# A Mamba scan kernel: the gates of the first two tiles share one table visit, and GpSimd's products use three places

## What is computed

```
xz = x @ win.T;  u, z = split(xz)                      # 1024 channels each
u = silu(conv4(u) + bconv);  dbc = u @ wx.T            # dt, B, C (16 states)
delta = softplus(dt @ wdt.T + bdt)
h = exp(delta * A) * h + (delta * u) * B_t             # a scan along the sequence, per channel and state
y = sum over the 16 states of h * C_t + u * Dp
y = (y * silu(z)) @ wout.T
```

## Time and profile before

| | |
|---|---|
| median of 3 runs | 7396.75 us (7392.23 to 7411.33) |
| the profiled execution, own time | 7406.93 us |
| its span, first to last instruction | 7405.0 us |
| busy share of the span | PE 91%, DVE 93%, ACT 83%, POOL 94% |
| granted TensorE clock, mean | 0.97 of full speed |
| share of the DMA engines | 46% |

### The profile page before, as it was taken

One profiled execution on the slowest core, in us unless ns is written; L12 is line 12 of the kernel. 1 busy time (PEld: TensorE's weight loads), 2 busy tenths in 40 slices (PEclk: granted clock), 3 DMA queues, 4 the chain that ended last, 5 costly groups with the idle time before them and its releaser, 6 DMA issues. The chain is left out here.

```text
span 7405.0 us, 108355 instructions
## 1 busy us (share of the span) xinstructions
PE 6731.3 (91%) x32416; PEld 4032.0 (54%) x32416; DVE 6877.8 (93%) x9234; ACT 6119.9 (83%) x13078; POOL 6953.7 (94%) x3764
## 2 busy tenths in 40 slices
PE   8999999999999999989999898999999999998799
PEld 5555555555555555555555555555555555555455
DVE  7999999999999999999999999999999999999766
ACT  6888888888888888888888888888888888888545
POOL 6999999999999999999999999999999999999678
PEclk9999999999999999999999999999999999999899
DMA  5455444445444444544444455344445544443155
GB/s 172 127 156 156 111 145 146 135 129 159 135 123 141 134 135 127 152 135 117 141 138 131 126 153 144 106 145 137 135 127 146 152 105 144 136 127 108 51 180 171
DMA packets 565933, 1006.64 MB, mean 136 GB/s; under 512 B 96624, under 2 KB 208368, under 8 KB 557552
## 3 DMA queue, kind: packets, MB, share of 16 engines
q1 hardware_dynamic: 559616, 993.54, 45.7%
q10 hardware_dynamic: 5744, 6.29, 0.3%
HBM read 875.49 MB, written 124.11 MB: 135 GB/s over the span
## 5 line engine op out<-in xcount | busy, mean ns | idle before, releaser
L517 POOL TENSOR_TENSOR dBu<-Bb,du 128x1024 f32<-128x1024 f32 x2048 | 4793.0, 2363 | 6.2 <-DMA Bb<-bc_scratch 4.7
L656 ACT ACTIVATE scans<-delta,A 128x512 f32<-128x512 f32 x4096 | 2745.0, 696 | 238.0 <-DVE hC L1160 216.6
L1144 DVE TENSOR_TENSOR_SCAN scans<-scans,state,dBu 128x512 f32<-128x512 f32 x2016 | 2533.4, 1277 | 228.5 <-ACT scans L656 224.0
L1144 DVE TENSOR_TENSOR_SCAN dBu<-scans,state,dBu 128x512 f32<-128x512 f32 x1568 | 1955.0, 1258 | 5.2 <-ACT scans L656 5.2
L892 PE MATMUL yT<-ident,hC 128*128 128x128 f32 x9216 | 1403.6, 283 | 289.0 <-DVE hC L1160 287.4
L1160 DVE TENSOR_TENSOR hC<-scans,Cb 128x512 f32<-128x512 f32 x2304 | 1551.0, 677 | 8.0 <-PE yT L892 7.8
L529 POOL TENSOR_TENSOR hR<-dBu,Cb 128x512 f32<-128x512 f32 x1024 | 1304.5, 1274 | 222.0 <-DVE dBu L1144 221.5
L892 PEld LDWEIGHTS yT<-ident,hC 128*128 128x128 f32 x9216 | 1087.2, 145 | 581.0 <-DVE hC L1160 364.6
L603 ACT ACTIVATE turned<-bg,CT 128x128 f32<-128x128 f32 x3072 | 875.0, 370 | 246.1 <-PE bg L869 245.7
L885 PE MATMUL bg<-u,comb 128*128 128x512 f32 x2048 | 963.6, 597 | 50.8 <-ACT pre L616 49.9
L843 PE MATMUL bg<-hT,win_z 128*128 128x512 f32 x2048 | 977.8, 600 | 0.0
(11 more groups left out here) (147 smaller groups left out, 7899.5 us busy)
## 6 DMA issues: line engine op xcount, KB each, us to landing
comb<-pre_scratch SPq DMA_DIRECT2D x992, 256.0 KB, 4.6
Bb<-bc_scratch SPq DMA_DIRECT2D x256, 512.0 KB, 6.9
Cb<-bc_scratch SPq DMA_DIRECT2D x256, 512.0 KB, 7.1
win_u<-in_win SPq DMA_DIRECT2D x256, 256.0 KB, 4.7
win_z<-in_win SPq DMA_DIRECT2D x256, 256.0 KB, 2.7
pre_scratch<-pre SPq DMA_DIRECT2D x248, 256.0 KB, 3.7
comb<-comb_scratch SPq DMA_DIRECT2D x61, 1024.0 KB, 7.2
part_scratch<-pre SPq DMA_DIRECT2D x128, 256.0 KB, 2.0
```

Source lines behind the costliest of these rows:

```text
L517: pool.tensor_tensor(dBu[:, ring(g, q)], Bb[:, 2 * q:2 * q + 2, :], du[:, j % 2, :].unsqueeze(1).broadcast_to([P, 2, T]), ALU.mult).then_i ...
L656: act.activation(place(n)[:], delta[:, j % 2, :], ACT.Exp, scale=A[:, i // CH_DIR, j * N + n:j * N + n + 1]).then_inc(dA_made, 1)
L1144: nc.vector.tensor_tensor_scan(to, place(n)[:], dBu[:, ring(g, q), k, :], state[:, c:c + 1] if i % CH_SEQ else 0.0, ALU.mult, ALU.add).the ...
```

## The change

z gets a second place. The z of tiles 0 and 1 go through silu together in the visit at position 7, and the visit at position 15 is gone. For that Z1 is done at positions 4 and 5, not 9 and 10, and the pieces of O0 to O3 are laid out anew. GpSimd's four products of a tile share three places in turn, not four of their own. The place in SBUF that the fourth one had served a load of wmod in the prologue too; this load now goes to Cb[8:12], so in the prologue the queue waits for the last prologue step before it loads the fifth pair of C. Nothing else in SyncE's order moves.

```diff
-HC, HR = 4, NA
+HC, HR = 4, 3
 GENERAL = [
-    ("D1", (0,), 0), ("Z0", (1, 2), 1), ("O0", (2, 2, 3, 3, 4, 4, 5, 5), 0), ("O1", (6, 6, 7, 7, 9, 9, 10, 10), 0),
-    ("D2", (7,), 1), ("Z1", (9, 10), 1), ("O2", (11, 11, 12, 12, 13, 13, 14, 14), 0), ("D3", (15,), 1),
-    ("O3", (15, 15, 17, 17, 18, 18, 19, 19), 0), ("Z2", (17, 18), 1), ("U0", (20, 20), 1), ("U1", (21, 21), 0),
+    ("D1", (0,), 0), ("Z0", (1, 2), 1), ("O0", (2, 3, 3, 4, 5, 6, 6, 7), 0), ("Z1", (4, 5), 1),
+    ("D2", (7,), 1), ("O1", (8, 8, 9, 9, 10, 10, 11, 11), 0), ("O2", (12, 12, 13, 13, 14, 14, 15, 15), 0), ("D3", (15,), 1),
+    ("O3", (16, 16, 17, 17, 18, 18, 19, 19), 0), ("Z2", (17, 18), 1), ("U0", (20, 20), 1), ("U1", (21, 21), 0),
-GATED = {7: (("Z", 0),), 15: (("Z", 1),), 23: (("Z", 2),), 31: (("C", 0), ("Z", 3)), 39: (("C", 2), ("Z", 4)),
+GATED = {7: (("Z", 0), ("Z", 1)), 23: (("Z", 2),), 31: (("C", 0), ("Z", 3)), 39: (("C", 2), ("Z", 4)),
-        z = sb("z", [P, T])
+        z = sb("z", [P, 2, T])
-        wgain = hR
+        wgain = Cb[:, 8:12]
+                    if last is None and q == 4:
+                        sp.wait_ge(bg_ready, PRO)
                     src = dram["bc"][s][N + 2 * q:N + 2 * q + 2, :].rearrange("n t -> (n t)")
                     sp.dma_start(Cb[:, 2 * q:2 * q + 2, :].rearrange("p n t -> p (n t)"),
-                                k = ASIDE.index(n)
+                                k = aside(g, n) % HR
                                 pool.wait_ge(h_made, g * N + n + 1 + H0)
                                 pool.wait_ge(hR_used, aside(g, n) + 1)
-                                if g == 0 and n == ASIDE[0]:
-                                    pool.wait_ge(bg_ready, PRO)
-            def take_z(made, bank, g):
+            def take_z(made, bank, tile):
                 act.wait_ge(bg_ready, made)
-                act.wait_ge(gated, g + 1)
-                act.copy(z[:], bank[:]).then_inc(bg_free, 1)
-            def silu_z(taken):
+                act.wait_ge(gated, max(tile, 1))
+                act.copy(z[:, tile % 2, :], bank[:]).then_inc(bg_free, 1)
+            def silu_z(taken, k):
                 act.wait_ge(bg_free, taken)
-                act.activation(z[:], z[:], ACT.Silu).then_inc(z_made, 1)
+                act.activation(z[:, k % 2, :], z[:, k % 2, :], ACT.Silu).then_inc(z_made, 1)
-                nc.vector.tensor_tensor(u[:, s, m, :], bank[:], z[:], ALU.mult).then_inc(gated, 1)
+                nc.vector.tensor_tensor(u[:, s, m, :], bank[:], z[:, m % 2, :], ALU.mult).then_inc(gated, 1)
```

More of the change, by code:

```diff
@@ L95 @@
 NUM_ACT = {name: e for e, name in enumerate(BY_ACT)}
-GATED = {7: (("Z", 0),), 15: (("Z", 1),), 23: (("Z", 2),), 31: (("C", 0), ("Z", 3)), 39: (("C", 2), ("Z", 4)),
+GATED = {7: (("Z", 0), ("Z", 1)), 23: (("Z", 2),), 31: (("C", 0), ("Z", 3)), 39: (("C", 2), ("Z", 4)),
          47: (("C", 4), ("Z", 5)), 53: (("C", 6), ("Z", 6)), 63: (("Z", 7),)}
-assert all(TAKE[f"{kind}{m + (kind == 'C')}"] < p + (kind == "Z") and (kind == "C" or p // NQ == m) for p in GATED for kind, m in GATED[p])
+assert all(TAKE[f"{kind}{m + (kind == 'C')}"] < p + (kind == "Z") and (kind == "C" or p // NQ <= m) for p in GATED for kind, m in GATED[p])
 assert sorted(m for p in GATED for kind, m in GATED[p] if kind == "C") == list(range(0, MT, 2))
@@ L691, in take @@
                 if kind == "Z":
-                    take_z(made, bank, g)
+                    take_z(made, bank, i * MT + k)
             nc.scalar.preload_act_table_set(SILU)
@@ L776, in _ @@
                                 if kind == "Z":
-                                    silu_z(freed(i, f"Z{k}"))
+                                    silu_z(freed(i, f"Z{k}"), k)
                             nc.scalar.preload_act_table_set(EXP_LN)
@@ L1021, in _ @@
                                 pe.wait_ge(hR_made, aside(g, n + 1))
-                                add_state(hR[:, ASIDE.index(n), :], False).then_inc(hR_used, 1)
+                                add_state(hR[:, aside(g, n) % HR, :], False).then_inc(hR_used, 1)
                         for n in (2 * q, 2 * q + 1):
```

## The result

| | before | after |
|---|---|---|
| median of 4 runs each | 7401.16 us (7392.23 to 7411.33) | 7482.35 us (7467.47 to 7492.57) |
| the profiled execution, own time | 7406.93 us | 7485.89 us |
| its span | 7405.0 us | 7484.1 us |

The ratio is 1.0114, with a 95% interval of 1.0101 to 1.0127: the kernel is slower, by 81 us. The forecast was 7449, with 7425 to 7475 as its own range and 7400 to 7490 for 8 runs in 10. The time lies outside the first and inside the second, in the part above 7475 that the prediction gave to its rival C (0.12).

The account below looks back on a forecast made before the run. TensorE's order of work sets ScalarE's visits, and these set VectorE. Late weights and the longer visit, less 1.2 us a chunk, gave +50, with chunks 0 and 31 +52: 7449 from a 7396.75 median; own range 7425 to 7475, 8 in 10 7400 to 7490.

Parts of the forecast that it names:

- rival C: TensorE's new waits lower its granted clock: 7499 if each chunk has a slow stretch, 7461 in a quarter; beyond 7475, chance 0.12.
- the place and the mechanism: At position 4, in L843, TensorE waits 1 to 3 us for the DMA of win_z in about half of the chunks.
- Rival B: The longer visit costs nothing at position 8 and the gain at position 21 remains: -43, time 7354; chance 0.09.
- The visit's own term: The visit at position 7 grows by Z1's take (0.589) and a second silu (0.623), less some overlap: 1.1 us.
- what is given back: With the visit at position 15 gone, a chunk gains 1.2 us from position 8 to position 21, not 1.40.
- three places at nothing: GpSimd waits 0.6 to 0.8 us for TensorE's hR add in tile 2 of every chunk, covered by idle time: cost 0.
- D: GpSimd's wait for TensorE's hR adds is not covered by its idle time: +25, time 7474; chance 0.08.
- Rival A: Z1's weights land after 2.7 us, in time, and a chunk loses 0.4 to 0.5: +8, time 7405; chance 0.14.
- the chunk: Chunks 1 to 30 lose 50 us: +2.5 in one like chunk 20, +0.5 to +2.1 in one like chunk 28.
- The two kinds of chunk become one: Normal and slow-start chunks become alike: T9 of tile 0 starts about 20.7 us after the first scan in nearly all.
- chunk 0: Chunk 0 has no O but the same wait for weights, landing 20.7 us after its first scan: +2, between -1 and 5.
- position 21: VectorE's wait at position 21, behind ScalarE's take of O3 at position 20, stays near 1.6 us.

Follow-up runs that it names:

- The first experiment: The changed kernel with win_z of tile 1 issued ahead of the last four pairs of B and C loads, except in chunk 0: 7413.94 us, 1.0019 of before.
- the third: The changed kernel with late weights kept, but z of tile 1 through silu at position 15 again: 7459.63 us, 1.008 of before.
- The last kernels: The changed kernel with early load, three O0 pieces behind T9, chunk 0's weights in the prologue: 7360.92 us; with the visit at 15 again: 7357.96 us.

## Why the prediction was right, and where its sizes were off

**Right: the place and the mechanism.** TensorE waits for the DMA of win_z in L843, 27 times in 32 chunks; 22 of the 30 middle chunks wait 1 us or more, where about half were forecast. The landings are 14.8 to 17.0 us behind the first scan, mean 15.8 (forecast: 15.6). VectorE's wait at positions 7 and 8 was to grow from 0.8 to about 4 us; it is 2.52 + 1.97 = 4.5. Those at 16 and 17 are zero. The first experiment shows the cause: with the weights in time, 68 of 81 us are gone. Rival B, faster because the visit costs nothing, is refuted by the first and the third: with the weights in time the kernel is no faster than before, and the second silu alone costs 0.51 at position 8. The visit's own term was 1.1, which is right for the visit itself: in chunk 20 it is 5.69 us from the copies of T9 to the exps behind the visit before (4423.40 to 4429.09), and 6.70 after (4482.73 to 4489.43). At the scan it was 0.4 too high: from T9 to position 8 the mean grew from 7.45 to 8.16, by 0.7.

**Right: what is given back.** From position 8 to position 21 the chunk was to gain 1.2 us. It took 69.67 - 26.06 = 43.61 before and takes 72.16 - 29.82 = 42.34: 1.27. It is not the visit that pays this back, as the text had it, since it is there with the visit at 15 too (71.31 - 28.98 = 42.33); what is left of the change are the O pieces moved away from TensorE's gap. No run moves them alone, so that they do it is argued and not shown.

**Right: three places at nothing.** D falls. GpSimd's new wait is 35.0 us in 43 waits, one a chunk and a few more, and the experiment with this part alone is at 1.0008 of before, with an interval that holds 1.

**Rival A's number, partly by luck.** A priced the change with the weights in time at 7405; measured, 7413.94, and 5.8 us between the two traces. It reached this by other terms than A's. Position 8 is late by 1.16 (27.22 and 26.06), where 1.6 to 1.7 was priced, and a chunk takes 0.08 more, where 0.45 was. Chunk 0 takes 230.3, 5.7 more than before, which A did not have. The other 8 us between the medians don't show in the traces.

**Too small: the chunk.** +1.66 was priced at position 21, +2.48 is measured. Two groups make it. The 22 chunks without a slow stretch at position 5 lose 1.83 each: T9 comes at 21.0, where 20.7 was forecast. The eight with one lose 4.27 each. That is 22 x 0.17 = 4 and 8 x 2.61 = 21 of the 25 us that are missing here. In the eight, Z1 begins 0.4 us later than in the others (16.21 and 15.80 behind the first scan) and T9 comes 2.3 later (23.38 and 21.04), so 1.9 arises between the two, at the lower clock. Two of the eight, chunks 18 and 24, have a low stretch twice as long as the others', with T9 at 25.1. This is rival C, in a quarter of the chunks; it had just that case at 7461, with 1.6 us for a stretch. The step that failed is the sum's assumption that TensorE runs at full clock behind its new wait. The range of 8 in 10 holds the time only because it reached into rival C.

"The two kinds of chunk become one" came true only for the old two. A new second kind arose: T9 at 20.2 to 22.3, and at 22.5 to 25.1.

**Too small: chunk 0.** +2 was priced (-1 to 5), +7.8 measured. TensorE in chunk 0 of after (first scan at 73.33), and two stretches there:

```profile
93.81 3.75 PE L843 MATMUL bg<-hT,win_z 128*128 128x512 f32 x4 [4.49 <-DMA win_z<-in_win]
97.35 1.06 PE L892 MATMUL yT<-ident,hR 128*128 128x128 f32 x4
...
100.62 0.60 PE L869 MATMUL bg<-ident,dBu 128*128 128x128 f32 x4
...
92.00:96.00 4.00, 2.19 (x3) 1.18 (x4) 4.00 (x6) 1.16 (x3) 3.92 (x4) 0.50 0.12 43
96.00:100.00 4.00, 4.00 (x13) 2.35 (x12) 2.72 (x5) 0.00 (x0) 2.62 (x3) 0.66 0.00 0
```

The landing was foretold to 0.3 us (20.7, and it is 93.81 - 73.33 = 20.5). What was not worked out is what stands behind it: a wait of 4.49, Z1's first half at half clock, and 1.88 for the second half ahead of T9, which so comes at 27.3. The term was set without the list of positions 4 and 5 that every other chunk was given. The last kernels confirm it: with this load moved too, chunk 0 is back at 225.0 us. The two terms that were too small make 25 + 6 = 31 us. The difference between the kernels is 81 us and was forecast at 52, so it is 29 short; in the traces the starts and ends give 3 back. The forecast time missed by 33, as 4 us more come from the median of before, which a fourth run moved from 7396.75 to 7401.16.

**Off by a little: position 21.** Its wait is 2.09, not 1.6. TensorE's list up to O3 has become no shorter, only the chunk ahead of it; so more of what is gained earlier is lost there (argued from the lists, not shown by a run). It is 2.1 in all kernels with the new layout, and the next thing to work on.

## What to carry to other kernels

When a step is moved forward, look where its operands are issued, not how long their loads take: a load whose median is 2.7 us landed 10.7 us after its issue in chunk 20 and 14.8 in chunk 0, because some 4 and 5.5 MB issued earlier in the same queue had not landed yet, and moving it forward in all chunks but chunk 0 was worth 68 us. Before two visits are merged to save a table load, ask which wait the saved one ends; here the new order had ended most of it already, and the longer visit was a cost at its new place. And put the work that ScalarE waits for (T9) ahead of the work that nobody waits for: that gave 1.65 us at position 8, 1.59 a chunk, and 52 us in all.

## What the runs showed of the hardware

TensorE's granted clock fell with a wait in the middle of a stretch that was full of work otherwise: 2.89 us of waiting in chunk 12, then 0.58 of the clock over 4 us; 4.49 us of waiting in chunk 0, and 0.50 and 0.66 over the 8 us from 92.0, which begin before that wait has ended. It did so in 8 of the 30 middle chunks, not in all that waited: chunk 20 waited 0.65 and kept 1.00, and so did chunk 11, which waited longer than chunk 12:

```profile
2509.92 1.96 PE L843 MATMUL bg<-hT,win_z 128*128 128x512 f32 x4 [3.09 <-DMA win_z<-in_win]
...
2510.00:2514.00 4.00, 4.00 (x16) 2.28 (x17) 4.00 (x6) 0.00 (x0) 4.00 (x4) 1.00 0.00 0
```

In chunk 12 it cost another half of the wait: 3.37 and not 1.88 us for the four matmuls behind it. Needless matmuls in the wait kept the clock up, but cure little, as they delay the real ones wherever the wait is shorter than they are.

A table load costs its 1283 ns and nothing around it that the rows show: all 224 of L772 have 4.0 us of idle time ahead of them together. A silu of 0.63 us more in a visit that VectorE waits for cost 0.51 us at position 8 in each chunk.
